# A graph attention kernel: score rows ordered by oct, attribute products as two 64-column tiles, weighted sums and transposes in one run each

## The chip, the cores and the metric

The kernel runs on one core of one Trainium2 chip. The metric is device time in microseconds. The kernel before takes 4986.42 us (median of 3 runs, 4981.60 to 4991.56). All numbers are fp32.

## The reference, cut to what matters

A graph of 6250 nodes and 206250 edges sorted by destination. One layer of attention over edges with 8 heads of 32 channels, then a feed-forward net, then a shared net and four gated experts.

```python
q, k, v = x @ Wq.T + bq, x @ Wk.T + bk, x @ Wv.T + bv       # per node, 8 heads x 32
e = edge_attr @ We.T                                        # per edge, from 64 attributes
alpha = sum(q[dst] * (k[src] + e), channels) / sqrt(32)     # 8 scores per edge
p = exp(alpha - segment_max(alpha, dst))
out = segment_sum((v[src] + e) * p, dst) / segment_sum(p, dst)
beta = sigmoid(concat(out, x_r, out - x_r) @ Wbeta.T)       # x_r: a skip projection
h = beta * x_r + (1 - beta) * out
x = layernorm(x + h); x = layernorm(x + gelu(x @ W1.T + b1) @ W2.T + b2)
y = x + shared_mlp(x) + gated top-2 of 4 experts
```

## The kernel before, in words

There are three stages. Stage 1 (to about 200 us) normalizes x, and makes for each node a row of keys and values in DRAM (`kv_rows`, 512 numbers) and columns of queries. Stage 2, the edge stage (about 200 to 3700 us), goes over 49 blocks of 128 nodes, and in each over GB = 8 steps of GN = 16 nodes. Stage 3 does everything behind the attention, row by row.

**One step of stage 2** has 16 nodes and their edges. The nodes are two octs of ON = 8; each oct (index `o`) has up to OW = 320 edges, so a step has 5 tiles of 128 edges. The edges' key and value rows are gathered by POOL, five indirect DMAs a step (L597), into one of four slots `F`; the edges' attributes and destination numbers come by SP's DMAs into `F3`.

TensorE does in a step:

- `scores` (L841, L844): for each half of the heads (index `c`) and each oct, 32 rows of scores (4 heads x 8 nodes) by 320 edges. Each is a product of queries with transposed keys `FT` and one of `G3` (queries times We) with the attributes `F3`, which also blanks edges of other nodes. The four row groups lie on four 32-wide column tiles of the array; in `pS` they stand at rows c*64 + o*32.
- `z_part` (L860), three times: for each of the four row groups the weights `PT` (32 columns) times 192 columns of `F`: 128 of values and the 64 attributes. To have these as one product for each half, the rows of `F` are laid out in blocks of 64: keys, a block of values, keys, values, values, values, attributes. It sums into `pZ`.
- `ft` (L828), three times: transposes of the keys of the step after the next, 4, 4 and 2, through the two buffers `ring`.
- `ea_rows` (L867): the next step's attributes with edges as rows. `pt` (L850): transposes of the weights `Pw`. `zt` (L873, L874): transposes of the sums `Zs` of the step, into `pZv` and `pZe`.

In step 1 of each block comes `project` (L881 to L887), in steps 2 and 5 `g3` (L818).

VectorE takes the maximum over `pS` (L656, L657), copies the transposed weights (L662), makes the blanking rows (L650), joins indices (L642), and twice a block takes `pZv` and `pZe` out (L678, L681). ScalarE copies `ring` to `FT` (L760), takes exp of the scores (L766), copies `pZ` to `Zs` (L807) and `pM` to `F` (L772). The order on each engine is written by hand, with semaphores between the engines: `ring_filled` and `ring_emptied` for ft, `s_done` for scores, `slot_free` for the last z of a step (POOL and SP start the loads of the next user of the slot on it), `z_out` for the copy of Z, `gathered` for a slot's rows.

## Time and profile before

| | |
|---|---|
| median of 3 runs | 4986.42 us (4981.60 to 4991.56) |
| profiled execution, whole time | 4956.95 us |
| its span | 4954.7 us |
| TensorE busy | 3986.7 us, 80% |
| VectorE, ScalarE, POOL busy | 1796.9, 1483.9, 1938.6 us |
| mean granted TensorE clock | 0.845 of full speed |
| gathers (L597) | 1970, 1894.3 us on POOL |

The profile is one execution of the program. A view in order of time gives start and length in us, the engine, the line of the kernel, the operation, the tiles written and read, shapes and the number of records put together; what stands in brackets is how long the engine had been idle and what released it. PE is TensorE, PEld its loads of weights, DVE VectorE, ACT ScalarE. A product in fp32 is two matmul records. The ends of TensorE's records are modelled.

### The profile page before, as it was taken

How to read it: one execution, taken by the hardware profiler on the slowest of the kernel's cores; microseconds unless marked ns; L12 is line 12 of the kernel's file. 1: busy time of each engine (PE TensorE's matmuls, PEld its weight loads, DVE VectorE, ACT ScalarE, POOL GpSimd, SP SyncE). 2: the span in 40 equal slices, each digit the busy share in tenths (PEclk: the TensorE clock that was granted, in tenths of full speed). 3: DMA queues.
4: the chain of work that ended last, by engine and by line, in shares of the span. 5: the costliest groups of instructions: out<-in, count | busy, mean ns of one | idle time of the engine just before them, and what ended most of it. 6: DMA issues, size and time to landing. Idle time of an engine off the chain costs nothing. (4 is left out here: it accounts for less than half of the span.)

```text
span 4954.7 us, 86461 instructions
## 1 busy us (share of the span) xinstructions
PE 3986.7 (80%) x28082; PEld 2157.7 (44%) x28082; DVE 1796.9 (36%) x4770; ACT 1483.9 (30%) x3644; POOL 1938.6 (39%) x2075
## 2 busy tenths in 40 slices
PE   6787888888888888888888888888867778778778
PEld 3344444444444444444444444444434445445445
DVE  5233333333333333333333333333335454544553
ACT  2133232222232233232332323223223323323322
POOL 2255555555555555555555555555530000000000
PEclk9788888888898888888889898888888778868877
DMA  5566666666666666666666666666660000000000
GB/s 191 161 180 179 172 172 172 175 170 169 181 179 172 168 176 170 173 174 173 173 171 182 178 183 179 172 171 177 170 165 18 15 15 15 15 15 15 15 15 7
DMA packets 638315, 665.65 MB, mean 134 GB/s; under 512 B 408275, under 2 KB 501908, under 8 KB 638244
## 3 DMA queue, kind: packets, MB, share of 16 engines
q0 software_dynamic: 159520, 523.41, 34.7%
q1 hardware_dynamic: 478740, 141.70, 13.9%
q14 instruction: 43, 0.35, 0.0%
q8 instruction: 12, 0.20, 0.0%
HBM read 632.59 MB, written 33.05 MB: 134 GB/s over the span
## 5 line engine op out<-in xcount | busy, mean ns | idle before, releaser
L597 POOL DMA_INDIRECT F<-kv_rows,srci x1970 | 1894.3, 962 | 1622.8 <-PE pZ L860 970.7
L760 ACT ACTIVATE FT<-ring 128x512 f32<-128x512 f32 (+1 forms) x1182 | 581.8, 526 | 1890.4 <-PE ring L828 1005.9
L828 PE MATMUL ring<-ident,F 128*128 128x128 f32 x3940 | 752.2, 309 | 407.8 <-ACT FT L760 392.5
L860 PE MATMUL pZ<-F,PT 128*32 128x192 f32 x9408 | 793.2, 362 | 117.6 <-issue 114.2
L828 PEld LDWEIGHTS ring<-ident,F 128*128 128x128 f32 x3940 | 447.1, 151 | 859.0 <-ACT FT L760 565.7
L656 DVE TENSOR_REDUCE nmx<-pS 128x1 f32<-128x384 f32 x393 | 219.3, 558 | 1263.3 <-remote 1098.9
L662 DVE COPY PT<-pPT 128x384 f32<-128x384 f32 x393 | 219.2, 558 | 956.6 <-issue 522.9
L860 PEld LDWEIGHTS pZ<-F,PT 128*32 128x32 f32 x9408 | 263.2, 116 | 483.0 <-issue 442.2
L1106 POOL DMA_DIRECT2D out_dram<-accb x6 | 5.8, 960 | 1077.8 <-DVEq L1271 1077.8
L841 PE MATMUL pS<-FT,qh 128*32 128x320 f32 x3144 | 382.6, 567 | 17.9 <-issue 14.2
L844 PE MATMUL pS<-F,G 80*32 80x320 f32 x3144 | 386.5, 571 | 0.0
L650 DVE TENSOR_SCALAR F<-F,nid 16x640 f32<-16x640 int32 x394 | 224.2, 569 | 41.5 <-issue 26.1
L850 PE MATMUL pPT<-ident,Pw 128*128 128x128 f32 x1179 | 236.0, 313 | 0.9 <-ACT Pw L766 0.9
L1382 PE MATMUL hid<-rT,W1T 128*128 128x512 f32 (+1 forms) x448 | 204.9, 617 | 35.6 <-ACT h L1314 27.9
L766 ACT ACTIVATE Pw<-pS,nMn 128x384 f32<-128x384 f32 x393 | 226.4, 576 | 7.6 <-DVE nMn L657 3.3
L778 ACT ACTIVATE G<-pM 64x512 f32<-64x512 f32 x99 | 58.6, 592 | 563.3 <-remote 380.6
L867 PE MATMUL pM<-ident,F 64*128 64x64 f32 x1965 | 213.5, 240 | 0.6
L844 PEld LDWEIGHTS pS<-F,G 80*32 80x32 f32 x3144 | 127.8, 140 | 171.9 <-issue 109.9
L1390 PE MATMUL nat<-W2T,h 128*128 128x256 f32 x784 | 176.3, 386 | 27.1 <-ACT h L1314 27.1
L867 PEld LDWEIGHTS pM<-ident,F 64*128 64x128 f32 x1965 | 158.2, 144 | 75.5 <-issue 75.5
L873 PE MATMUL pZv<-ident,Zs 128*128 128x128 f32 x392 | 137.8, 351 | 63.4 <-issue 55.0
L1287 ACT ACTIVATE rT<-tr 128x256 f32<-128x256 f32 x147 | 54.4, 384 | 436.8 <-PE tr L1373 434.9
(200 smaller groups left out, 4427.7 us busy)
## 6 DMA issues: line engine op xcount, KB each, us to landing
F<-in_edge_attrT SPq DMA_DIRECT2D x788, 80.0 KB
F<-kv_rows,srci POOLq DMA_INDIRECT x1970
F<-in_dst SPq DMA_DIRECT2D x788, 20.0 KB
srci<-src_front SPq DMA_DIRECT2D x796, 1.5 KB
kv_rows<-kvs SPq DMA_DIRECT2D x7, 1792.0 KB, 6.4
qb<-q_cols SPq DMA_DIRECT2D x100, 64.0 KB
U<-in_x SPq DMA_DIRECT2D x7, 896.0 KB, 10.9
xn_rows<-xs SPq DMA_DIRECT2D x7, 896.0 KB, 6.3
```

What stands on the lines that cost most here:

```text
L597: pool.indirect_dma_start(out=F[s][:, t, 0:KV], out_offset=None, in_=kv_d, in_offset=bass.IndirectOffsetOnAxis(ap=srci[j % GB][:, col:col ...
L650: dve.tensor_scalar(F3[j][DE:K3, :], F3[j][DE:K3, :].bitcast(I32), nid[DE:K3, c], None, ALU.not_equal).then_inc(neq_done, 1)
L656: ch.step(dve.tensor_reduce(nmx[:, j:j + 1], pS[:, 0:SW], AX.X, ALU.max, negate=True))
L662: dve.tensor_copy(PT[:, :, :], pPT[:, 0:SW].rearrange("p (t r) -> p t r", r=P)).then_inc(pt_emptied, 1)
L760: act.activation(FT[j % 2][:, :, t0 * P:t1 * P], ring[n % 2][:, 0:KD * w].rearrange("p (k e) -> p k e", e=w), ACT.Copy).then_inc(ring_empt ...
L766: act.activation(Pw[:, :], pS[:, 0:SW], ACT.Exp, bias=nMn[:, j:j + 1], accum_out=lsum[:, j:j + 1]).then_inc(p_done, 1)
L828: m = pe.transpose(ring[n % 2][:, k * w + (t - t0) * P:k * w + (t - t0 + 1) * P], F[j][:, t, k * 3 * BLK:k * 3 * BLK + P], ident[:, :])
L841: m = pe.matmul(pS[rows, cols], qh[half][:, c, g + o, :], FT[j % 2][:, c, o * OW:(o + 1) * OW], start=True, stop=False)
L844: m = pe.matmul(pS[rows, cols], G3[half][0:K3, c, g + o, :], F3[s][0:K3, o * OW:(o + 1) * OW], start=False, stop=True)
L850: m = pe.transpose(pPT[:, t * P:(t + 1) * P], Pw[:, t * P:(t + 1) * P], ident[:, :])
L860: m = pe.matmul(pZ[rows, 0:ZW].rearrange("p (x d) -> p x d", d=BLK), PT[:, t, rows], f, start=(t == 0), stop=(t == KB - 1))
L867: m = pe.transpose(pM[:, t * DE:(t + 1) * DE], F3[s][0:DE, t * P:(t + 1) * P], ident[0:DE, 0:DE])
```

## The change

Four things change together, and no arithmetic is left out.

- Row groups of scores, weights and sums stand at rows o*64 + c*32 in place of c*64 + o*32: first by oct, then by half of the heads. `seln`, `selh`, `G3`, the blanks and the reads of `pZv` and `pZe` follow.
- The two row groups of an oct are then neighbours and use the same attributes. The products with attributes, in `scores` and in `z_part`, are two on 64-wide column tiles in place of four on 32-wide ones. In `z_part` the values are four products of 128 columns, and the attributes two of 64 columns; before, both were in four of 192.
- The layout of a gathered row is keys (256), values (256), attributes (64), in place of blocks in turn, with fewer DMAs of weights and biases in stage 1.
- On TensorE all three `z_part` come first, then the three `ft`; the wait for gathered rows moves behind the sums. On ScalarE exp comes first, then the copy of `pZ`, then the three copies of `ring`.

```diff
--- before.py
+++ after.py
@@ -138,7 +137,7 @@
             nid = sbt(mid, "nid", [P, NG + 2])
-            G3 = [sbt(mid, f"G3{i}", [P, KD, HP // ON, C]) for i in range(2)]
+            G3 = [sbt(mid, f"G3{i}", [P, HP // ON, KD, C]) for i in range(2)]
             WeP = sbt(mid, "WeP", [P, HR, 2 * C])
@@ -205,16 +204,12 @@
                         wv = a["WvT"].rearrange("(k p) c -> p k c", p=P)
-                        for at, v0, v1 in ((2, 0, 1), (5, 1, 2), (6, 2, 4)):
-                            sp.dma_start(Wkv[:, :, at * BLK:(at + v1 - v0) * BLK], wv[:, :, v0 * BLK:v1 * BLK]).then_inc(wv_landed, 16)
-                            sp.dma_start(bkv[:, at * BLK:(at + v1 - v0) * BLK], a["bv"][v0 * BLK:v1 * BLK].partition_broadcast(P)
-                                         ).then_inc(bias_landed, 16)
+                        sp.dma_start(Wkv[:, :, D:KV], wv).then_inc(wv_landed, 16)
+                        sp.dma_start(bkv[:, D:KV], a["bv"].partition_broadcast(P)).then_inc(bias_landed, 16)
                         sp.dma_start(src_d[HP:], a["src"]).then_inc(src_stored, 16)
...
                         sp.wait_ge(bk_stored, 16)
-                        for o in range(KD):
-                            sp.dma_start(bkv[:, o * 3 * BLK:o * 3 * BLK + P], bk_d[o * P:(o + 1) * P].partition_broadcast(P)
-                                         ).then_inc(bias_landed, 16)
+                        sp.dma_start(bkv[:, 0:D], bk_d.partition_broadcast(P)).then_inc(bias_landed, 16)
                         sp.wait_ge(wep_cleared, 1)
@@ -279,7 +274,7 @@
                                         out=selh[:, c * HR:(c + 1) * HR], in_=selh[:, c * HR:(c + 1) * HR],
-                                        compare_op=ALU.not_equal, fill=1.0, base=-(c * HP + o * C + n),
+                                        compare_op=ALU.not_equal, fill=1.0, base=-(o * HP + c * C + n),
                                         pattern=[[-ON, HR]], channel_multiplier=1))
@@ -294,9 +289,11 @@
                                 for h in range(HR):
-                                    g3 = G3[i][:, :, :, :].rearrange("p c (g o) r -> p (c g) o r", o=2)[:, :, o, h * ON:(h + 1) * ON]
-                                    chp.step(pool.affine_select(out=g3, in_=g3, compare_op=ALU.not_equal, fill=-BIG, base=-(DE + o * ON),
-                                                                pattern=[[0, KD * HP // GN], [-1, ON]], channel_multiplier=1))
+                                    for c in range(KD):
+                                        g3 = G3[i][:, :, c, :].rearrange("p (g o) r -> p g o r", o=2)[:, :, o, h * ON:(h + 1) * ON]
+                                        chp.step(pool.affine_select(out=g3, in_=g3, compare_op=ALU.not_equal, fill=-BIG,
+                                                                    base=-(DE + o * ON), pattern=[[0, HP // GN], [-1, ON]],
+                                                                    channel_multiplier=1))
                         pool.sem_inc(sel_ready, 1)
@@ -621,9 +617,7 @@
                         for o in range(2):
-                            for c in range(KD):
-                                r = c * HP + o * C
-                                dve.memset(pS[r:r + C, (1 - o) * OW:(1 - o) * OW + HP], -BIG).then_inc(blank, 1)
+                            dve.memset(pS[o * HP:(o + 1) * HP, (1 - o) * OW:(1 - o) * OW + HP], -BIG).then_inc(blank, 1)
                         dve.memset(pZv[:, :], 0.0).then_inc(blank, 1)
@@ -676,10 +670,10 @@
                                 dve.tensor_copy(outT[rows, :, half, :].rearrange("p c (x n) -> p c x n", n=ON),
-                                                pZv[rows, :].rearrange("p (c x h n) -> p c x h n", c=KD, h=HR, n=ON)[:, :, :, h, :])
+                                                pZv[rows, :].rearrange("p (x c h n) -> p c x h n", c=KD, h=HR, n=ON)[:, :, :, h, :])
                             for c in range(KD):
                                 m = dve.tensor_copy(zeaT[c * DE:(c + 1) * DE, :, half, :].rearrange("p h (x n) -> p x h n", n=ON),
-                                                    pZe[0:DE, :].rearrange("p (c x h n) -> p c x h n", c=KD, h=HR, n=ON)[:, c, :, :, :])
+                                                    pZe[0:DE, :].rearrange("p (x c h n) -> p c x h n", c=KD, h=HR, n=ON)[:, c, :, :, :])
                             m.then_inc(copied, 1)
@@ -775,7 +769,8 @@
                             act.wait_ge(g3_filled, value)
-                            act.activation(G3[half][0:DE, :, :, :].rearrange("p c x r -> p (c x r)"), pM[0:DE, :], ACT.Copy
+                            act.activation(G3[half][0:DE, :, :, :].rearrange("p x c r -> p c x r"),
+                                           pM[0:DE, :].rearrange("p (c x r) -> p c x r", c=KD, r=C), ACT.Copy
                                            ).then_inc(g3_emptied, 1)
@@ -798,13 +793,12 @@
                                         g3_out(0, it * 2 + 3)
+                                    weights((j + 1) % GB, it * GB + (j + 2))
+                                    act.wait_ge(slot_free, it * GB + (SLOTS + j + 1))
+                                    act.activation(Zs[:, :], pZ[:, 0:ZW], ACT.Copy).then_inc(z_out, 1)
                                     for q in range(len(PAIRS)):
...
                                         ft_out(j, q, RING0 + m, rb + (m + 1))
-                                        if q == 0:
-                                            weights((j + 1) % GB, it * GB + (j + 2))
-                                    act.wait_ge(slot_free, it * GB + (SLOTS + j + 1))
-                                    act.activation(Zs[:, :], pZ[:, 0:ZW], ACT.Copy).then_inc(z_out, 1)
                                     ea_out((j + 1) % SLOTS, it * GB + (j + 2))
@@ -826,23 +820,21 @@
                                     m = pe.transpose(ring[n % 2][:, k * w + (t - t0) * P:k * w + (t - t0 + 1) * P],
-                                                     F[j][:, t, k * 3 * BLK:k * 3 * BLK + P], ident[:, :])
+                                                     F[j][:, t, k * P:(k + 1) * P], ident[:, :])
                             m.then_inc(ring_filled, 1)
...
                             half, g = j // HB, (j % HB) * 2
-                            for x in range(2):
-                                for c in range(KD):
-                                    for o in range(2):
-                                        r = c * HP + o * C
-                                        rows, cols = slice(r, r + C), slice(o * HP, o * HP + OW)
-                                        if x == 0:
-                                            m = pe.matmul(pS[rows, cols], qh[half][:, c, g + o, :],
-                                                          FT[j % 2][:, c, o * OW:(o + 1) * OW], start=True, stop=False)
-                                        else:
-                                            m = pe.matmul(pS[rows, cols], G3[half][0:K3, c, g + o, :],
-                                                          F3[s][0:K3, o * OW:(o + 1) * OW], start=False, stop=True)
+                            for c in range(KD):
+                                for o in range(2):
+                                    r = o * HP + c * C
+                                    pe.matmul(pS[r:r + C, o * HP:o * HP + OW], qh[half][:, c, g + o, :],
+                                              FT[j % 2][:, c, o * OW:(o + 1) * OW], start=True, stop=False)
+                            for o in range(2):
+                                m = pe.matmul(pS[o * HP:(o + 1) * HP, o * HP:o * HP + OW],
+                                              G3[half][0:K3, g + o, :, :].rearrange("p c r -> p (c r)"),
+                                              F3[s][0:K3, o * OW:(o + 1) * OW], start=False, stop=True)
                             m.then_inc(s_done, 1)
@@ -854,11 +846,12 @@
                                 for o in range(2):
-                                    rows = slice(c * HP + o * C, c * HP + (o + 1) * C)
-                                    blocks = F[s][:, o * TO + t, :].rearrange("p (x d) -> p x d", d=BLK)
-                                    f = blocks[:, 2:9:3, :] if c == 0 else blocks[:, 6:9, :]
-                                    m = pe.matmul(pZ[rows, 0:ZW].rearrange("p (x d) -> p x d", d=BLK), PT[:, t, rows], f,
-                                                  start=(t == 0), stop=(t == KB - 1))
+                                    rows = slice(o * HP + c * C, o * HP + (c + 1) * C)
+                                    pe.matmul(pZ[rows, 0:P], PT[:, t, rows], F[s][:, o * TO + t, D + c * P:D + (c + 1) * P],
+                                              start=(t == 0), stop=False)
+                            for o in range(2):
+                                rows = slice(o * HP, (o + 1) * HP)
+                                m = pe.matmul(pZ[rows, P:ZW], PT[:, t, rows], F[s][:, o * TO + t, KV:FP], start=False, stop=(t == KB - 1))
                             return m
@@ -869,9 +862,9 @@
 
-                            g = slice((j % HB) * HP, (j % HB + 1) * HP)
-                            pe.transpose(pZv[:, :].rearrange("p (c r) -> p c r", c=KD)[:, :, g], Zs[:, 0:P], ident[:, :])
-                            pe.transpose(pZe[0:DE, :].rearrange("p (c r) -> p c r", c=KD)[:, :, g], Zs[:, P:ZW], ident[:, :]).then_inc(zt_filled, 1)
+                            g = slice((j % HB) * P, (j % HB + 1) * P)
+                            pe.transpose(pZv[:, g], Zs[:, 0:P], ident[:, :])
+                            pe.transpose(pZe[0:DE, g], Zs[:, P:ZW], ident[:, :]).then_inc(zt_filled, 1)
 
@@ -941,12 +934,12 @@
                                         z = z_part(s, t)
-                                        if t == KB - 1:
-                                            z.then_inc(slot_free, 1)
-                                        if t == 0:
-                                            pe.wait_ge(gathered[s2], it * (16 * T * 2) + 16 * T * ((j + 2) // SLOTS + 1))
-                                        pe.wait_ge(ring_emptied, rb + (m + t - 1))
-                                        ft(s2, t, RING0 + m + t)
+                                    z.then_inc(slot_free, 1)
+
+                                    pe.wait_ge(gathered[s2], it * (16 * T * 2) + 16 * T * ((j + 2) // SLOTS + 1))
+                                    for q in range(len(PAIRS)):
+                                        pe.wait_ge(ring_emptied, rb + (m + q - 1))
+                                        ft(s2, q, RING0 + m + q)
                                     if j == 1:
```

TensorE's instructions for one step without extra work (step 3 of a block), before. `pS` are scores, `pZ` sums, `ring` the transposed keys, `pM` the attribute rows, `pPT` the transposed weights; 32x320 is a product's output.

```order
L841 MATMUL pS<-FT,qh 32x320 x4
L844 MATMUL pS<-F,G 32x320 x4
L860 MATMUL pZ<-F,PT 32x192 x4
...
L828 MATMUL ring<-ident,F 128x128 x4
L860 MATMUL pZ<-F,PT 32x192 x4
L828 MATMUL ring<-ident,F 128x128 x4
L860 MATMUL pZ<-F,PT 32x192 x4
...
L828 MATMUL ring<-ident,F 128x128 x2
L867 MATMUL pM<-ident,F 128x64 x5
L850 MATMUL pPT<-ident,Pw 128x128 x3
L873 MATMUL pZv<-ident,Zs 128x2x64
L874 MATMUL pZe<-ident,Zs 64x2x64
```

After:

```order
L832 MATMUL pS<-FT,qh 32x320 x4
L835 MATMUL pS<-F,G 64x320 x2
L850 MATMUL pZ<-F,PT 32x128 x4
L854 MATMUL pZ<-F,PT 64x64 x2
L850 MATMUL pZ<-F,PT 32x128 x4
L854 MATMUL pZ<-F,PT 64x64 x2
L850 MATMUL pZ<-F,PT 32x128 x4
L854 MATMUL pZ<-F,PT 64x64 x2
...
L822 MATMUL ring<-ident,F 128x128 x8
...
L822 MATMUL ring<-ident,F 128x128 x2
L860 MATMUL pM<-ident,F 128x64 x5
L842 MATMUL pPT<-ident,Pw 128x128 x3
L866 MATMUL pZv<-ident,Zs 128x128
L867 MATMUL pZe<-ident,Zs 64x128
```

Each z has its two attribute products behind the value products, the three z stand in one run, and eight of the ten transposes of keys follow in one run.

ScalarE's instructions of the same step, before:

```order
L760 ACTIVATE FT<-ring 128x2x256
L766 ACTIVATE Pw,lsum<-pS,nMn 128x384
...
L760 ACTIVATE FT<-ring 128x2x256
...
L760 ACTIVATE FT<-ring 128x2x128
...
L807 ACTIVATE Zs<-pZ 128x192
L772 ACTIVATE F<-pM 128x5x64
```

After:

```order
L760 ACTIVATE Pw,lsum<-pS,nMn 128x384
...
L798 ACTIVATE Zs<-pZ 128x192
...
L754 ACTIVATE FT<-ring 128x2x256
...
L754 ACTIVATE FT<-ring 128x2x256
...
L754 ACTIVATE FT<-ring 128x2x128
L766 ACTIVATE F<-pM 128x5x64
```

exp (`Pw`) and the copy of the sums (`Zs`) moved ahead of the copies of `ring` into `FT`.

## Rows read from the trace of the kernel before

**Rows 1.** The page's first line on busy time: engine, us, share of the span, instructions.

```profile
PE 3986.7 (80%) x28082; PEld 2157.7 (44%) x28082; DVE 1796.9 (36%) x4770; ACT 1483.9 (30%) x3644; POOL 1938.6 (39%) x2075
```

**Rows 2.** Busy time by stretch: the edge stage, and the step of rows 3 (clock granted).

```profile
800.00:3600.00 2800.00, 2325.42 (x20026) 1185.28 (x20019) 888.37 (x2495) 840.19 (x2338) 1526.16 (x1588) 0.87 0.64 174
...
2029.40:2043.00 13.60, 9.93 (x104) 5.26 (x104) 5.90 (x17) 4.94 (x14) 7.20 (x9) 1.00 0.65 179
```

**Rows 3.** TensorE in order of time, one step: start, length, line, operation, idle before.

```profile
2034.54 0.74 PE L841 MATMUL pS<-FT,qh 128*32 128x320 f32 x8
2035.10 0.72 PE L844 MATMUL pS<-F,G 80*32 80x320 f32 x8
2035.64 0.51 PE L860 MATMUL pZ<-F,PT 128*32 128x192 f32 x8
2036.08 0.66 PE L828 MATMUL ring<-ident,F 128*128 128x128 f32 x4
2036.66 0.53 PE L860 MATMUL pZ<-F,PT 128*32 128x192 f32 x8
...
2037.71 0.53 PE L860 MATMUL pZ<-F,PT 128*32 128x192 f32 x8
2040.87 0.44 PE L828 MATMUL ring<-ident,F 128*128 128x128 f32 x2 [2.62 <-ACT FT L760]
...
2041.69 0.55 PE L850 MATMUL pPT<-ident,Pw 128*128 128x128 f32 x3
2042.51 0.30 PE L873 MATMUL pZv<-ident,Zs 128*128 128x128 f32 x1 [0.27 <-issue]
...
2042.85 0.59 PE L841 MATMUL pS<-FT,qh 128*32 128x320 f32 x4
```

**Rows 4.** VectorE in order of time, the same step.

```profile
2037.32 0.56 DVE L656 TENSOR_REDUCE nmx<-pS 128x1 f32<-128x384 f32 x1 [2.09 <-PE pS L844]
2037.91 0.16 DVE L657 TENSOR_TENSOR nMn<-nmx,nMo 128x1 f32<-128x1 f32 x1
```

**Rows 5.** ScalarE in order of time, the same step.

```profile
2040.22 0.60 ACT L760 ACTIVATE FT<-ring 128x512 f32<-128x512 f32 x1 [5.78 <-remote]
2040.71 0.57 ACT L766 ACTIVATE Pw<-pS,nMn 128x384 f32<-128x384 f32 x1
2041.18 0.20 ACT L766 ACTIVATION_READ_ACCUMULATOR Pw<-pS,nMn 128x1 f32 x1
2041.27 0.87 ACT L760 ACTIVATE FT<-ring 128x512 f32<-128x512 f32 x2
2042.01 0.35 ACT L807 ACTIVATE Zs<-pZ 128x192 f32<-128x192 f32 x1
```

**Rows 6.** POOL in order of time, the first gather after the same step's sums.

```profile
2041.29 0.94 POOL L597 DMA_INDIRECT F<-kv_rows,srci  x1 [2.24 <-remote]
```

**Rows 7.** The page's costliest groups: the maximum, one for each step.

```profile
L656 DVE TENSOR_REDUCE nmx<-pS 128x1 f32<-128x384 f32 x393 | 219.3, 558 | 1263.3 <-remote 1098.9
```

**Rows 8.** Groups by line and shape, 800 to 3600 us: busy, mean ns, idle before.

```profile
L656 DVE TENSOR_REDUCE nmx<-pS 128x1 f32<-128x384 f32 x317 | 176.9, 558 | 1022.7 <-remote 908.1 <-PE pS L844 78.3 <-issue 36.3
...
L884 PE MATMUL pM<-WeP,zeaT 128*128 128x64 f32 x320 | 56.3, 339 | 0.0
...
L874 PEld LDWEIGHTS pZe<-ident,Zs 128*64 128x64 f32 x317 | 40.2, 127 | 0.0
```

**Rows 9.** All engines in order of time, a step whose scores are delivered late.

```profile
1349.76 0.75 PE L841 MATMUL pS<-FT,qh 128*32 128x320 f32 x8
...
1355.45 0.56 DVE L656 TENSOR_REDUCE nmx<-pS 128x1 f32<-128x384 f32 x1 [3.85 <-remote]
1355.57 0.60 ACT L760 ACTIVATE FT<-ring 128x512 f32<-128x512 f32 x1 [5.90 <-PE ring L828]
...
1358.74 0.76 PE L841 MATMUL pS<-FT,qh 128*32 128x320 f32 x4
```

**Rows 10.** POOL in order of time, its first long wait at the start.

```profile
90.49 1.64 POOL L305 MEMSET U<- 128x1848 f32 x1 [10.69 <-DVE xs L344]
```

14 lines of the change are left out of this document (6 added, 8 removed).

## The prediction

> **What bounds the kernel now.** I read the page's shares first: TensorE is busy for 80% of the span, every other engine under 40% [rows 1]. The stretch 800 to 3600 us is all edge stage; DMA engines are busy 64% there, POOL 55% [rows 2]. So neither moves all the time, and the question is what TensorE's stretch of one step consists of. The edge stage is 392 steps of 16 nodes (393 maxima with the one ahead of the loop [rows 3]); 317 of them lie in 2800 us, 8.83 us each on average [rows 2, 4], so it is seven tenths of the time.
>
> Next I read one step in order of time without extra work, at the full clock [rows 2, 5]. Scores start at 2034.54 and the next scores at 2042.85: 8.31 us. TensorE's records of scores and the three weighted sums (z) with two runs of row transposes between them (ft) end by 2038.24, 3.7 us after the start. Then it stands still for 2.62 us and goes on with the third ft, edge rows, transposes of the weights (pt) and of the sums (zt), and the next scores. What it waits for is ScalarE's copy of the first ft, which starts at 2040.22 [rows 6]. So ScalarE's first copy is in the chain. It wasn't late because of other work on ScalarE: ScalarE had been idle for 5.78 us.
>
> The third reading is how late the other engines see what TensorE's records call finished. The score records end at 2035.82, and DVE's maximum, which waits for nothing else, starts at 2037.32 [rows 7]: 1.5 us later. The first ft's records end at 2036.74, and the copy starts 3.5 us later. POOL, which waits for the last z (records end 2038.24), goes on at 2041.29 [rows 8]. After transposes alone there is no such gap: pt ends at 2042.24 and its copy on DVE follows at once. So the column-tiled products deliver late, and results come together: the copy of ft at 2040.22 and POOL's restart are a microsecond apart though a z, an ft and another z lie between. I call the stretch from the start of scores to 2040.22 the head (5.68 us) and the rest the tail (2.63 us).
>
> By the Trainium skill (Perfetto Trace Analysis, Tensor Engine Instruction), TensorE's end in a profile is estimated from the instruction's size, not observed. The trace agrees: after tiled products, waiting engines start 1.5 to 3.5 us behind that end. So I size the head by when others start, not by TensorE's busy time.
>
> The tail: the ft copy (0.60) lets the third ft start at 2040.87; then edge rows; pt 2041.69; zt at 2042.51, held 0.27 us for the copy of Z, which starts at 2042.01 because exp and the three ft copies are ahead of it [rows 5, 6].
>
> **The change part by part**, per step.
>
> Term 1, z products. Before, each of three z is four products of 192 columns on 32-wide tiles, each run as two matmuls (eight records). After, it is four of 128 columns and two of 64 columns on 64-wide tiles: twelve records. Four records of 320 columns side by side take a quarter of 2034.54 to 2035.64, 0.275 us [rows 5], 0.86 ns a column. Sixty-four fewer columns in two rounds save 0.11 us per z, 0.33 in all. The added products: at least the same columns on two tiles, 0.11 per z, net 0. At most each of four stands alone for 0.18 us, what a 64-column matmul with full-width weights takes (56.3 us by 320 [rows 4]): 0.70 per z, net +1.8. The nearest row for the weights is the 64-wide load, 0.127 us [rows 4]; two rounds of that, pairs side by side, are 0.26 per z: net +0.45. I take this. The score products against the attributes go from four to two on 64-wide tiles with the same 320 columns, so two rounds stay two rounds: nothing.
>
> Term 2, changes between tile shapes. z to ft start to start takes 0.44 us for 192 columns in two rounds, 0.33 by the above; ft to the next z 0.58 for four transposes of 0.11 (four last 0.66, three of pt 0.55): 0.11 to 0.15 us lost at each change, 0.13 on average. Between scores and third ft there are five changes. After: if 32-wide to 64-wide counts as a change, there are eight (two around the attribute scores, five within z, one to ft): +3, +0.39. If it doesn't, only one is left: -4, -0.5. No row shows 32 against 64. I take +0.39, since the weights of the one shape occupy the array that the other needs.
>
> The Trainium skill (TensorEngine Tiling (Array Packing), Key Properties) says that a change of the tiling mode, not just of the tile, drains TensorE. The trace agrees for 32 to 128 wide, 0.13 us each; by the rule 32 to 64 would cost likewise, which is the upper of the two counts and speaks against this change.
>
> Term 3, order in the head. Before, the ft copy comes as late as the whole run z, ft, z, ft, z. After, it needs three z and one ft; the second ft runs beside ScalarE's copies of Z (0.35) and of the first ft (0.60). One ft of 0.58 us leaves the head: -0.58 at best. At worst nothing, if the late delivery sets the head. I take -0.58.
>
> Term 4, tail. ScalarE now does exp, Z copy, three ft copies. The Z copy waits for the last z and runs beside the first ft. zt no longer waits: -0.27. pt doesn't wait either, exp being long done. In the tail edge rows and pt stay in the chain.
>
> Term 5, late scores. exp (ready 0.75 after the maximum starts, then 0.67 with its read) now stands ahead of every ft copy. In the step shown the maximum starts at 2037.32 and exp would be over at 2038.8, before the last z is delivered: free. But there are steps where scores are delivered with everything else [rows 9]: scores from 1349.76, maximum at 1355.45, ft copy at 1355.57, next scores 1358.74. There exp runs behind the first copy today. After, the minimum is ready at 1356.20, exp with its read at about 1356.9, Z copy 1357.24, ft copy 1357.84 instead of 1356.17: +1.67, and from there 1.75 instead of 2.57: net +0.85. DVE's mean wait ahead of the maximum is 3.23 us over 317 steps (1022.7 us), between the 2.09 of the first step and 3.85 of the late one [rows 4, 7, 9]. After, 36 tiled matmul records follow the scores with nothing between; before, transposes came after eight. I see no reason why scores be delivered earlier, some why later, and count half of the steps: +0.45. Ends 0 and +0.85.
>
> The rest: POOL's 16 added selects at the start run ahead of a wait of 10.69 us for x rows [rows 10], which would have to grow past that to show; covered. Eight DMAs of weights and biases become three; the matmuls of that stage wait for the rows of x longer. The gathers wait for the last z and are needed two steps on: 6.3 us of issue in 8.3 leave room, and TensorE asks for them later than before. Strided reads on DVE and ScalarE keep their sizes. Stage 3 is the same code.
>
> Sum: +0.45 +0.39 -0.58 -0.27 +0.45 = +0.44 us a step, by 392 steps +172 us. The profiled execution is 4956.95 us (span 4954.7), 29 below the median 4986.42 of the runs: 5129 against the profile, 5158 against the runs. I say 5150.
>
> **The rivals.**
> - Faster, order alone counts: 32 against 64 is no change of mode and the added products hide at their columns: 0 -0.5 -0.58 -0.27, with late steps at +0.45: -0.9 us a step, at most -350 us; if delivery, not issue, sets the head, half of it, about 4800. For it: TensorE stands 2.62 us in wait of a copy. Against: that copy isn't late through order, but through delivery. It decides from the point at which the six z and attribute groups cost under 0.15 us a step more than today.
> - Slower by the count of tiled products: the head is the same in slow and fast steps where records are 3.7 us long, as if each tiled matmul had a price in delivery. There are 40 in the 5.68 us, 0.14 each; after, 48: +1.1 us a step, +445, about 5420. For it: results come late only behind tiled products. Against: maybe width counts, and the 64-wide ones are fewer bytes.
> - No change: the head is set by something outside (gathers' traffic beside it) and what the tail wins the late steps lose: 4986.
>
> **How the numbers follow.** My forecast, slower by one to six per cent: 0.5. Count of tiled products: 0.17. Faster: 0.25. No change: 0.08. What a measurement can tell from no change is 0.2%, 10 us. So faster 0.25, same 0.07, slower 0.68. The likeliest case's own range is 5030 to 5300. The range that holds 8 in 10 goes from 4840 (leaving out the best of the faster case) to 5400.
>
> **What would show it.** In the profile after: the step without extras at 8.7 to 8.8 us, from 8.3; the first attribute product of z 0.13 us or more behind the records' columns (term 2); twelve records per z in about 0.75 us (terms 1 and 2); ScalarE in the order exp, Z, ft; zt right behind pt (term 4); steps in which Z's copy begins right behind exp (term 5). I am wrong if z with its attribute products takes no longer than today, or if ScalarE's first ft copy begins earlier than 5.5 us after the scores.

## The result and the profile after

The changed kernel takes 5033.26 us (median of 4 runs, 5024.53 to 5035.17) against 4984.01 us of before on the same chip (4959.93 to 4991.56): ratio 1.0104, 95% interval 1.0067 to 1.0140. It is slower, as forecast, but by 49 us where I had forecast 166. Measured again on another chip (e9 below), both kernels were equal (1.0010, 0.9993 to 1.0027).

Groups of rows are named here by the numbers under which they stand above. (The prediction numbers six of them otherwise: its 3 is Rows 7, its 4 is Rows 8, its 5 is Rows 3, its 6 is Rows 5, its 7 is Rows 4, its 8 is Rows 6.)

The page's first line, after; [rows 1] of before. The span is 5022.5 us, 67.8 longer.

```profile
PE 4135.4 (82%) x31214; PEld 2452.8 (49%) x31214; DVE 1795.1 (36%) x4768; ACT 1597.7 (32%) x3644; POOL 1945.9 (39%) x2091
```

Busy time by stretch, after: the edge stage, then two steps that follow each other. Columns as in [rows 2]: stretch and length; TensorE, its loads, VectorE, ScalarE, POOL; clock, DMA share, GB/s.

```profile
800.00:3600.00 2800.00, 2390.27 (x22120) 1396.85 (x22123) 871.80 (x2451) 918.46 (x2301) 1500.90 (x1558) 0.88 0.63 171
...
2014.10:2023.00 8.90, 7.35 (x80) 3.92 (x80) 4.29 (x14) 2.78 (x8) 4.90 (x6) 1.00 0.63 173
2023.00:2032.00 9.00, 7.54 (x64) 4.50 (x66) 3.79 (x11) 2.83 (x7) 4.64 (x6) 0.81 0.62 167
```

TensorE is busy 65 us longer in the 2800 us, with fewer steps done; the clock and the traffic stayed. TensorE in order of time, after, a step without extra work at the full clock; it answers to [rows 3].

```profile
2014.14 0.75 PE L832 MATMUL pS<-FT,qh 128*32 128x320 f32 x8
2014.82 0.76 PE L835 MATMUL pS<-F,G 80*64 80x320 f32 x4
2015.51 0.43 PE L850 MATMUL pZ<-F,PT 128*32 128x128 f32 x8
2015.86 0.34 PE L854 MATMUL pZ<-F,PT 128*64 128x64 f32 x4
2016.13 0.42 PE L850 MATMUL pZ<-F,PT 128*32 128x128 f32 x8
2016.48 0.34 PE L854 MATMUL pZ<-F,PT 128*64 128x64 f32 x4
2016.90 0.27 PE L850 MATMUL pZ<-F,PT 128*32 128x128 f32 x1
2017.65 0.27 PE L850 MATMUL pZ<-F,PT 128*32 128x128 f32 x1 [0.48 <-issue]
2018.36 0.45 PE L850 MATMUL pZ<-F,PT 128*32 128x128 f32 x6 [0.44 <-issue]
2018.74 0.34 PE L854 MATMUL pZ<-F,PT 128*64 128x64 f32 x4
2019.01 1.09 PE L822 MATMUL ring<-ident,F 128*128 128x128 f32 x8
2020.64 0.44 PE L822 MATMUL ring<-ident,F 128*128 128x128 f32 x2 [0.55 <-ACT FT L754]
2021.01 0.52 PE L860 MATMUL pM<-ident,F 64*128 64x64 f32 x5
2021.46 0.55 PE L842 MATMUL pPT<-ident,Pw 128*128 128x128 f32 x3
2021.85 0.27 PE L866 MATMUL pZv<-ident,Zs 128*128 128x128 f32 x1
...
2022.16 0.75 PE L832 MATMUL pS<-FT,qh 128*32 128x320 f32 x8
```

This step takes 8.02 us, less than the 8.31 of [rows 3]; the next one, at a mean clock of 0.81 of full speed (partly at 1.2 GHz), 9.58. One step is no mean, which matters below. The first two sums start 0.62 us apart (2015.51, 2016.13), where z to ft took 0.44. The scores take 1.37 us to the first sum, 1.10 before. Then TensorE issues single records some 0.7 us apart, until 2018.36: the stop that stood behind the third z is now within it.

VectorE, ScalarE and POOL in order of time, the same step; [rows 4 to 6].

```profile
2018.42 0.56 DVE L650 TENSOR_REDUCE nmx<-pS 128x1 f32<-128x384 f32 x1 [1.88 <-remote]
```

```profile
2019.21 0.58 ACT L760 ACTIVATE Pw<-pS,nMn 128x384 f32<-128x384 f32 x1 [5.39 <-DVE nMn L651]
2019.69 0.19 ACT L760 ACTIVATION_READ_ACCUMULATOR Pw<-pS,nMn 128x1 f32 x1
2019.78 0.32 ACT L798 ACTIVATE Zs<-pZ 128x192 f32<-128x192 f32 x1
2019.99 1.51 ACT L754 ACTIVATE FT<-ring 128x512 f32<-128x512 f32 x3
```

```profile
2016.29 0.95 POOL L593 DMA_INDIRECT F<-kv_rows,srci  x1 [0.30 <-issue]
2019.97 0.94 POOL L593 DMA_INDIRECT F<-kv_rows,srci  x1 [2.73 <-PE pZ L854]
```

The first of the two is the last of the five gathers that POOL had begun behind the step before. The same one of the kernel before, in the step of [rows 3]:

```profile
2038.10 0.94 POOL L597 DMA_INDIRECT F<-kv_rows,srci  x1 [0.30 <-issue]
```

The score records end at 2015.58 and the maximum starts 2.84 us later. ScalarE now waits for it; the copy of Z begins right behind exp, and the first ft copy after that, 5.85 us behind the start of the scores (5.68 before).

Groups by line, after, 800 to 3600 us: the maximum ([rows 8]), exp and the copy of Z.

```profile
L650 DVE TENSOR_REDUCE nmx<-pS 128x1 f32<-128x384 f32 x312 | 174.0, 558 | 956.6 <-remote 840.9 <-PE pS L835 110.1 <-issue 5.6
...
L760 ACT ACTIVATE Pw<-pS,nMn 128x384 f32<-128x384 f32 x312 | 180.7, 579 | 1269.6 <-DVE nMn L651 1083.9 <-issue 178.8
...
L798 ACT ACTIVATE Zs<-pZ 128x192 f32<-128x192 f32 x312 | 100.9, 323 | 73.2 <-PE pZ L854 72.2
```

VectorE's wait ahead of the maximum is 3.07 us a step (3.23 before). The copy of Z waits only 0.23 us a step; in 224 of the 312 steps it begins right behind exp, where I had counted such a delay in half of the steps.

### The profile page after: what moved, and what is told of

The parts are those of the page before. It is cut to its first block and busy times, and to the rows that moved or that the text cites. A ratio compares the mean times of both kernels' runs of the same rounds, so it can differ in the third digit from the quotient of the medians.

```text
span 5022.5 us, 92750 instructions
## 1 busy us (share of the span) xinstructions
PE 4135.4 (82%) x31214; PEld 2452.8 (49%) x31214; DVE 1795.1 (36%) x4768; ACT 1597.7 (32%) x3644; POOL 1945.9 (39%) x2091
## 5 line engine op out<-in xcount | busy, mean ns | idle before, releaser
L850 PE MATMUL pZ<-F,PT 128*32 128x128 f32 x9408 | 668.3, 296 | 251.4 <-issue 245.8
L822 PEld LDWEIGHTS ring<-ident,F 128*128 128x128 f32 x3940 | 526.0, 168 | 245.4 <-ACT FT L754 185.6
L854 PE MATMUL pZ<-F,PT 128*64 128x64 f32 x4704 | 476.0, 257 | 160.5 <-issue 157.9
L850 PEld LDWEIGHTS pZ<-F,PT 128*32 128x32 f32 x9408 | 247.2, 110 | 581.2 <-issue 529.2
L854 PEld LDWEIGHTS pZ<-F,PT 128*64 128x64 f32 x4704 | 276.7, 143 | 436.9 <-issue 431.9
L832 PE MATMUL pS<-FT,qh 128*32 128x320 f32 x3144 | 327.8, 493 | 1.2 <-issue 0.7
L835 PE MATMUL pS<-F,G 80*64 80x320 f32 x1572 | 321.3, 489 | 0.0
L860 PE MATMUL pM<-ident,F 64*128 64x64 f32 x1965 | 236.5, 259 | 0.0
L860 PEld LDWEIGHTS pM<-ident,F 64*128 64x128 f32 x1965 | 177.4, 161 | 89.8 <-issue 89.8
L835 PEld LDWEIGHTS pS<-F,G 80*64 80x64 f32 x1572 | 82.0, 142 | 235.6 <-issue 235.6
```

What stands on the lines that cost most here:

```text
L822: m = pe.transpose(ring[n % 2][:, k * w + (t - t0) * P:k * w + (t - t0 + 1) * P], F[j][:, t, k * P:(k + 1) * P], ident[:, :])
L832: pe.matmul(pS[r:r + C, o * HP:o * HP + OW], qh[half][:, c, g + o, :], FT[j % 2][:, c, o * OW:(o + 1) * OW], start=True, stop=False)
L835: m = pe.matmul(pS[o * HP:(o + 1) * HP, o * HP:o * HP + OW], G3[half][0:K3, g + o, :, :].rearrange("p c r -> p (c r)"), F3[s][0:K3, o * OW ...
L850: pe.matmul(pZ[rows, 0:P], PT[:, t, rows], F[s][:, o * TO + t, D + c * P:D + (c + 1) * P], start=(t == 0), stop=False)
L854: m = pe.matmul(pZ[rows, P:ZW], PT[:, t, rows], F[s][:, o * TO + t, KV:FP], start=False, stop=(t == KB - 1))
L860: m = pe.transpose(pM[:, t * DE:(t + 1) * DE], F3[s][0:DE, t * P:(t + 1) * P], ident[0:DE, 0:DE])
```

## The experiments

Eighteen runs in five groups, each group on one chip beside the kernel before. "Mean step" is the time from one step's scores to the next in the trace (360 to 383 steps, 300 to 3650 us): of all, of the five of a block without extra work, of the three with `project` or `g3`. The first line is the result itself.

| kernel | median us | ratio to before (95%) | mean step: all / without / with extra |
|---|---|---|---|
| before | 4984.01 | 1 | 8.81 / 8.46 / 9.38 |
| changed | 5033.26 | 1.0104 (1.0067–1.0140) | 8.97 / 9.04 / 8.87 |
| e1 old tiles, both new orders | 4845.04 | 0.9783 (0.9756–0.9810) | 8.52 / 8.44 / 8.64 |
| e2 new tiles, both old orders | 5110.54 | 1.0310 (1.0272–1.0348) | 9.26 / 9.16 / 9.41 |
| e3 ScalarE's new order alone | 5030.87 | 1.0169 (1.0138–1.0200) | 8.97 / 8.72 / 9.40 |
| e4 TensorE's new order alone | 4796.87 | 0.9707 (0.9672–0.9743) | 8.39 / 8.26 / 8.60 |
| e9 changed again | 4945.91 | 1.0010 (0.9993–1.0027) | 8.77 / 8.87 / 8.59 |
| e10 = e4 again | 4800.06 | 0.9705 (0.9690–0.9721) | 8.37 / 8.25 / 8.57 |
| e11 attribute sums together | 4894.70 | 0.9893 (0.9871–0.9915) | 8.64 / 8.65 / 8.63 |
| e12 two ft ahead of the sums | 4871.53 | 0.9845 (0.9831–0.9860) | 8.60 / 8.35 / 9.02 |
| e13 changed, ScalarE's old order | 4871.26 | 0.9845 (0.9832–0.9859) | 8.58 / 8.48 / 8.74 |
| e14 changed, scores 32-wide | 5000.25 | 1.0100 (1.0083–1.0116) | 8.93 / 9.01 / 8.80 |
| e15 changed, sums 32-wide | 4962.81 | 1.0025 (1.0001–1.0049) | 8.80 / 8.91 / 8.62 |
| e16 before, one gather a step | 3768.94 | 0.7616 (0.7604–0.7628) | 5.76 / 5.26 / 6.59 |
| e17 sums of 192 columns, ScalarE's old order | 4816.54 | 0.9665 (0.9636–0.9694) | 8.48 / 8.26 / 8.84 |
| e18 sums of 192 columns | 4947.76 | 0.9939 (0.9916–0.9962) | 8.74 / 8.44 / 9.24 |

e5 to e8 ran on a chip on which the kernel before takes 4081.66 us; they stand apart below. e1 to e4 shared a chip (before 4953.85), e9 to e12 another (4947.48), e13 to e16 a third (4948.54); e17 and e18 ran later on that one (4977.84). Ratios of different groups are compared below; where two such ratios differ by less than about 1%, I don't read the difference, since e9 and the first line are the same kernel and differ by 0.9%.

**Orders against tiles.** e1 takes both of these parts from the change, e4 TensorE's alone, e3 ScalarE's alone; e2 is the changed kernel with both undone.

```diff
 TensorE:
-for t in range(KB): z_part(s, t); (t == 0: wait gathered); ft(s2, t)
+for t in range(KB): z_part(s, t)
+wait gathered
+for q in range(3): ft(s2, q)
 ScalarE:
-ft copy 0, exp, ft copy 1, ft copy 2, wait slot_free, Zs<-pZ
+exp, wait slot_free, Zs<-pZ, ft copies 0, 1, 2
```

Expected of e1: 

> The kernel before with the two orders of the change (TensorE: three z, then three ft; ScalarE: exp, copy of Z, ft copies), tiles and layout as before. Theory A, the order is what costs: exp stands ahead of the ft copies in steps whose scores are delivered late, 0.85 us in some of them, so this kernel is slower than before by all of the change's 49 us or more, 5030 to 5080. Rival B, the tiles cost (64-wide products in between 32-wide ones) and the order gains, since one ft leaves the chain and zt waits no more: faster than before, 4880 to 4970.

Of e2: 

> The changed kernel with both orders put back (z and ft in turn; first ft copy, exp, the other ft copies, copy of Z); row order, layout and the 64-wide attribute products stay. Theory A (order costs): about as before, 4960 to 5000. Rival B (tiles cost): slower than the changed kernel, 5050 to 5150, because between every two ft there are two more changes of tile shape.

Of e3: 

> The kernel before with ScalarE's order alone changed (exp, copy of Z, then the ft copies). TensorE's order is as before, so the first ft copy additionally waits for the last z, exp and the copy of Z. Theory A: this alone is the loss, 5050 to 5200, as ft copies are 0.35 us later in each step and 1.7 us in late ones. Rival B: as ft and z are delivered together anyway, 0 to +30 us.

Of e4: 

> The kernel before with TensorE's order alone changed (z, z, z, then ft, ft, ft); ScalarE as before (first ft copy, exp, two ft copies, copy of Z). If three z in one run lengthen nothing, the first ft copy comes as late as now and time is unchanged within 20 us (both theories allow it); if delivery of scores is held by a run of tiled products without transposes between, the steps get longer, +50 us or more; if changes between tile shapes cost 0.13 us each, four fewer give -200 us.

TensorE's order gains 2.9%, ScalarE's loses 1.7% alone and 0.8% behind TensorE's (e1 against e4), the tiles lose 3.1%. So the change joins a gain with two losses. Of the expectations only one held: e2 lies where rival B had it. e1 is faster than both of its ranges, e3 with +77 us lies between its two, and e4's -157 us is nearest to the price for changes of tile shape, which later runs don't bear out.

**The same on a quick chip.** e5, e6 and e7 are the changed kernel with one edit:

```diff
 e5, scores:
-for o: pe.matmul(pS[o*HP:(o+1)*HP, ...], G3[..., g+o] as 64 columns, F3)
+for c: for o: pe.matmul(pS[r:r+C, ...], G3[..., g+o, c, :], F3)
 e6, z_part:
-for o: pe.matmul(pZ[o*HP:(o+1)*HP, P:ZW], ...)
+for c: for o: pe.matmul(pZ[o*HP+c*C:o*HP+(c+1)*C, P:ZW], ...)
 e7: the 12 value products of a step, then the 6 attribute products
 e8 (before): POOL gathers one tile of five in the loop
```

In e8 four slots are filled whole ahead of the loop, and most edges then use rows of earlier steps: it leaves out four fifths of the gathers.

Expected of e5: 

> The changed kernel with the attribute scores on four 32-wide tiles again (the attribute products of z stay two on 64-wide tiles). Two of eight changes of tile shape a step go. Theory S, a change of shape between 32 and 64 wide costs about 0.13 us: 2 by 0.13 by 392 = 100 us faster than the changed kernel, 4900 to 4930. Rival N, the number of tiled products counts (48 records a step become 52): 20 to 80 us slower than it, 5020 to 5090.

Of e6: 

> The changed kernel with the attribute products of z on four 32-wide tiles of 64 columns (eight records in place of four for each z), scores as changed. Six changes of shape a step go to one, 12 more records come. Theory S: at least 5 by 0.13 by 392 = 250 us faster than the changed kernel, about 4750, if the records themselves are free. Rival N (records count, 0.14 us each by the prediction's sum): 12 more, +600 us, 5600; a result near the changed kernel's would say that both weigh alike.

Of e7: 

> The changed kernel with the 12 value products of a step's z first and then the six 64-wide attribute products, same records, in place of value and attribute products in turn. Changes of shape within z go from six to two. Theory S: 4 by 0.13 by 392 = 200 us faster than the changed kernel, 4790 to 4840. Rival N: unchanged, within 15 us of it, since the number of records is the same.

Of e8: 

> The kernel before with one of the five gathers of a step in the loop (four slots are filled whole ahead of it); so most edges use the rows of earlier steps, and the gathered traffic and POOL's work fall to a fifth. It asks what delays the delivery of tiled products. Theory D, the gathers' traffic does: VectorE's wait ahead of the maximum falls from 3.2 us a step to under 1.5, and the kernel takes 4000 to 4500 us. Rival E, it lies in the tiled products themselves at the full clock: the wait stays at 3 us and the time within 2% of before.

Medians 4008.84, 3971.53, 3971.30 and 3763.94 us; ratios 0.9826 (0.9786–0.9865), 0.9740 (0.9701–0.9780), 0.9738 (0.9699–0.9777) and 0.9228 (0.9180–0.9276). The mean step of e7 is 6.32 us. Its window of the edge stage, the maximum there, and TensorE in one step:

```profile
800.00:2600.00 1800.00, 1642.69 (x20277) 1052.56 (x20279) 801.18 (x2255) 847.87 (x2105) 1364.63 (x1428) 1.00 0.86 244
```

```profile
L650 DVE TENSOR_REDUCE nmx<-pS 128x1 f32<-128x384 f32 x286 | 159.5, 558 | 83.1 <-PE pS L835 79.5
```

```profile
2006.87 0.86 PE L853 MATMUL pZ<-F,PT 128*32 128x128 f32 x24
2007.66 0.57 PE L858 MATMUL pZ<-F,PT 128*64 128x64 f32 x12
2008.16 1.09 PE L822 MATMUL ring<-ident,F 128*128 128x128 f32 x8
```

VectorE waits 0.29 us a step ahead of the maximum here, not 3: the scores aren't delivered late. POOL starts its 1428 gathers 1.26 us apart with pauses of 0.30 us, so five take 6.30 us, and they bound the step. So this chip couldn't tell the terms apart in time, and e8 couldn't test what makes delivery late. It does show one price of issue: the three z of e7 take 1.29 us to the first ft, and three of 0.62 us would take 1.86, so four changes of tile width fewer save 0.57 us, 0.14 each. The kernel before wasn't profiled on this chip.

**Again where delivery is late.** e9 is the changed kernel, e10 is e4, e11 is e7. e12 is before with this order on TensorE (ScalarE: ft, ft, exp, ft, Z):

```diff
-z_part 0, ft 0, z_part 1, ft 1, z_part 2, ft 2
+ft 0, ft 1, z_part 0, z_part 1, z_part 2, ft 2
```

Expected of e9: 

> The changed kernel itself, once more. The same kernel before took 4954 us on one chip and 4082 us on another, where VectorE waits 0.2 us ahead of the maximum in place of 3.2. Where results of tiled products are delivered late, the ratio to before should be 1.010 again. Where they aren't, theory S (changes of shape cost what the records show) and the order's gain leave it below before: e5 and e6, which differ from it by two and five changes of shape, were at 0.983 and 0.974, so 0.98 to 1.00.

Of e10: 

> The kernel before with TensorE's order alone changed, which was at 0.971 of before on a chip with late delivery. On such a chip again 0.971. On one without, POOL's five gathers (6.27 us a step) bound the step, and it comes to 0.97 too, like e7 (3971 us), by another cause; theory S says not above 0.98 on either.

Of e11: 

> The changed kernel with the values of all three z first and then their attribute products (e7), for the other kind of chip. With late delivery theory S says 200 us faster than the changed kernel (four changes of shape a step), a ratio to before of 0.96 to 0.975; theory N (the number of tiled records counts there) says the same as the changed kernel, 1.00 to 1.015.

Of e12: 

> The tiles of before, with the first two runs of transposes ahead of the three z and the third behind them; ScalarE copies the first two, then does exp, the third copy and the copy of Z. The third ft then waits for no copy and the first copy starts about 2 us earlier. Where the first ft copy is in the chain (late delivery) faster than e10: 0.94 to 0.97. If the delivery of everything behind the scores is held until the window of tiled products has drained, it is the same as e10, 0.97. Where gathers bound, the same as e10 within 0.5%.

e10 repeats e4 to 0.0002. e11, with four changes of tile shape fewer, is 51 us faster than the changed kernel, 0.03 us a change; that lies between its two theories. The changed kernel was expected at 1.010 again and came at 1.001. In e12, ft ahead of the sums is worse than behind them (0.9845 against 0.9705), outside all that I had expected of it, and the runs don't say why.

**Which tile edit, and ScalarE's order with new tiles.** e13 is the changed kernel with ScalarE's old order, e14 is e5, e15 is e6, e16 is e8.

Expected of e13: 

> New tiles, TensorE's new order, ScalarE's old order. If the two parts add (order of TensorE alone 0.971 of before, new tiles alone +3.1%): about 1.00. If ScalarE's new order costs what it cost with the old tiles (+1 to +1.7%), this is 0.985 to 0.99 of before where the changed kernel is 1.00 to 1.01. If the tiles' cost lies where the old order changes shape twelve times and not in the z run, it is 0.975 or less.

Of e14: 

> The changed kernel with its attribute scores on four 32-wide tiles again: two changes of shape fewer a step. My term: -0.26 us a step, 100 us, 0.98 of the changed kernel. By the grouping run (four changes fewer, -51 us): -25 us, 0.995. Rival, price by matmuls: two matmuls more, +50 us.

Of e15: 

> The changed kernel with its attribute sums on four 32-wide tiles of 64 columns: six changes fewer a step, six matmuls more. By my terms -0.78 us a step, at most -300 us. By the grouping run -75 us. Rival, price by matmuls: at least +150 us.

Of e16: 

> The kernel before with one of five gathers a step in the loop; most edges then use rows of earlier steps. If the gathers' traffic is what makes scores arrive late, VectorE's mean wait ahead of the maximum falls from 3.2 us to under 1 and the time to 0.85 or less. If it is not, the wait stays above 2.5 us and the time at 0.97 or more.

e13 beats the changed kernel by 1.65% (0.9845 against e9's 1.0010) and loses 1.4% to e10. In this order of taking parts ScalarE's order is the larger loss; by e1 and e4 it was 0.8%, and the tiles then 2.3 to 3.3% (e9 and the first line against e1). Which of the two is larger depends on what else is in place. TensorE in order of time in e14:

```profile
2002.67 0.75 PE L832 MATMUL pS<-FT,qh 128*32 128x320 f32 x8
2003.23 0.72 PE L837 MATMUL pS<-F,G 80*32 80x320 f32 x8
2003.77 0.40 PE L851 MATMUL pZ<-F,PT 128*32 128x128 f32 x8
```

and in e15:

```profile
2000.24 0.45 PE L850 MATMUL pZ<-F,PT 128*32 128x128 f32 x8
2000.48 0.33 PE L855 MATMUL pZ<-F,PT 128*32 128x64 f32 x8
2000.59 0.43 PE L850 MATMUL pZ<-F,PT 128*32 128x128 f32 x8
2000.81 0.33 PE L855 MATMUL pZ<-F,PT 128*32 128x64 f32 x8
2001.07 1.09 PE L822 MATMUL ring<-ident,F 128*128 128x128 f32 x8
```

In e14 the scores take 1.10 us again, 0.27 less than with two 64-wide products: 0.13 us for each of two changes of tile width. In e15 a z takes 0.35 us, and 0.48 with the change to ft behind it, not 0.62. Neither shortened the kernel: 1.0100 and 1.0025, where the changed one has 1.0010 to 1.0104. So the time doesn't pay for TensorE's issue in the head one for one. Both forecasts for e14 and both for e15 missed. e14 is 54 us slower than e9, close to the 50 of the price by matmuls, but on another chip; e15, of which that price asked at least 150, is 17 us slower.

e16, the kernel before with a fifth of the gathers, in the same views: window, the maximum's group, TensorE, VectorE, ScalarE. Its edge stage ends at 2486 us, so the window is shorter.

```profile
800.00:2400.00 1600.00, 1587.96 (x17512) 893.37 (x17508) 768.93 (x2188) 763.12 (x2051) 263.42 (x278) 1.00 0.39 85
```

```profile
L658 DVE TENSOR_REDUCE nmx<-pS 128x1 f32<-128x384 f32 x278 | 155.0, 558 | 71.1 <-PE pS L846 70.0
```

```profile
2003.34 0.75 PE L843 MATMUL pS<-FT,qh 128*32 128x320 f32 x8
2003.91 0.72 PE L846 MATMUL pS<-F,G 80*32 80x320 f32 x8
...
2008.50 0.48 PE L843 MATMUL pS<-FT,qh 128*32 128x320 f32 x4
```

```profile
2004.70 0.56 DVE L658 TENSOR_REDUCE nmx<-pS 128x1 f32<-128x384 f32 x1 [0.27 <-PE pS L846]
```

```profile
2005.58 0.60 ACT L762 ACTIVATE FT<-ring 128x512 f32<-128x512 f32 x1 [2.34 <-PE ring L830]
```

The wait ahead of the maximum is 0.26 us (3.23 with all gathers), the first ft copy comes 2.24 us behind the start of the scores (5.68), and the step takes 5.16 us (8.31) with the same products in the same order. TensorE is busy for 99% of the window. Without most of the gathers this chip and the quick one are alike: 3768.94 and 3763.94 us. So the gathers make delivery late. e16 takes away their transfers and POOL's work of issuing them together, so it doesn't say which of the two.

**The split of the sums.** e18 is the changed kernel with rows laid out in blocks and a z of four products of 192 columns, as before; e17 has ScalarE's old order as well.

```diff
-values: 4 x 128 columns (32-wide), attributes: 2 x 64 columns (64-wide)
+4 x 192 columns (32-wide), F in blocks of 64 as before
```

TensorE in e17, the three sums in one run and the first ft behind them:

```profile
2000.46 1.18 PE L859 MATMUL pZ<-F,PT 128*32 128x192 f32 x24
2001.58 0.66 PE L829 MATMUL ring<-ident,F 128*128 128x128 f32 x4
```

Expected of e17: 

> The sums with their attributes in one product of 192 columns as before (rows laid out as before); attribute scores on two 64-wide tiles, rows by oct, TensorE's new order, ScalarE's old order. With new sums this was 0.9845 of before, with old tiles throughout 0.9705. If the sums' split costs the 70 us between them: 0.970 here. If the attribute scores do: 0.984. Per my term 1 the sums' split costs +0.45 us a step, and this would be 0.95 of before.

Of e18: 

> The same with ScalarE's new order, so the changed kernel but for the split of the sums. The changed kernel was 1.001 to 1.010 of before, the new orders with old tiles 0.978. If the split makes the difference: 0.978 to 0.99. If it is the attribute scores: 1.00.

The split costs 1.8% with ScalarE's old order (e13 against e17), by the ratios some 89 us or 0.23 us a step; the two medians, from different groups on one chip, are 55 us apart. Without it, e17 is at e10's level (0.9665 and 0.9705, in different groups), near the 0.970 that was expected if the split costs; there the 64-wide scores cost nothing that I can show. With ScalarE's new order they do: e18 is 1.6% above e1 (0.9939 and 0.9783, on different chips), and outside both ranges expected of it. e18 against e17 gives ScalarE's order 131 us. e17 and e4/e10 beat both kernels; which of the two is better stays open.

## Why the forecast had the sign and not the size

The parts don't add up in one way. Three walks through the mean steps lead from before (8.81) to the changed kernel (8.97, or 8.77 in the second trace, whose differences stand in brackets).

| part, us a step | through e4, e13 | through e4, e1 | through e2, e13 | forecast |
|---|---|---|---|---|
| tiles | +0.19 | +0.45 (+0.25) | +0.45 | +0.84 |
| TensorE's order | -0.42 | -0.42 | -0.68 | -0.58 |
| ScalarE's order | +0.39 (+0.19) | +0.13 | +0.39 (+0.19) | +0.18 |

Each sums to +0.16 or -0.04, by 392 steps +63 or -16 us. On every walk the tiles are what was sized most wrongly.

- **Terms 1 and 2 (tiles), +0.84: the step that failed.** It failed in two places.
  - As issue of TensorE, term 2 was right: about 0.13 us for each change, eight for five, +0.39. Term 1 was not. In e17 three z of 192 columns in a run take 1.12 us to the first ft, one change among it, so 0.33 each; the 0.62 of the changed z has two changes in it and leaves 0.36. The added products cost 0.03 us a z, 0.1 a step, and not the +0.45 that I took from a row on loads of weights. "Twelve records per z in about 0.75 us" came as 0.62.
  - Of this issue the time pays a part. From e4 to e13 the tiles add seven changes and the 0.1, some 1.0 us of issue, and the mean step grows by 0.19; from before to e2 they add 0.78 (0.27 in the scores, 0.17 in each z), and it grows by 0.45. e14 and e15 show it from the other side: 0.27 and some 0.7 us a step of issue taken out, nothing gained. I had put the whole of it on the path, though my own reading was that the head is set by late delivery and must be sized by when others start. By the Trainium skill (TensorEngine Tiling (Array Packing), Key Properties) a change of mode drains TensorE; the trace agrees that 32 to 64 wide loses time as 32 to 128 does, 0.13 us each, but the kernel's time shows 0.03 us of it in e11.
- **The path, which I had wrong too.** Of the gathers I wrote that 6.3 us of issue in 8.3 leave room. In the traces they don't. In all 340 steps of before between 400 and 3400 us POOL issues its five gathers in one run of 6.0 us, then stands until the last z is delivered, 2.78 us on average; 6.0 and 2.8 are the mean step. In 271 steps of before ScalarE had waited over 1 us for its first ft copy, and in none of them did the copy start while such a run went on; the median start is 1.23 us behind the run's end (1.03 to 1.40 in eight of ten). In the step of [rows 3] the fifth gather ends at 2039.04 and the copy starts at 2040.22, and in the changed kernel the fifth ends at 2017.24 and the maximum starts at 2018.42: 1.18 us both times. So most results look held until the gathers are out, and what lengthens the step is what is still missing of z at that time. POOL's mean stand is 2.32 us in e4, 2.42 in e17, 2.41 in e13, 2.53 in e1, 2.93 in the changed kernel and 3.21 in e2, nearly in step with the mean steps. In the step shown only two of the third z's twelve records are out before 2018.36, and POOL stands 2.73 us; in the step of before all three z were out by 2038.24, and it stood 2.25. That this is how the tiles cost their part is my reading of one step each, and that the gathers hold the results is argued from these times and from e16; no run moved or stretched the gathers alone. Some results do get through during the run: 247 of the 340 maxima of before start within it.
- **Term 3 (order on TensorE), -0.58:** right in kind, -0.42 to -0.68. Its 0.58 for one ft contains a change of tile shape (0.44 without), which term 2 had already taken out, so my sum counted that 0.14 twice. The gain isn't even over the steps: -0.20 without extra work, -0.78 with `project` or `g3` (e4).
- **Terms 4 and 5 (ScalarE), -0.27 and +0.45, net +0.18:** right in sign; measured +0.13 with the old tiles (e4 to e1), +0.19 and +0.39 with the new ones. I had counted half of the steps, and exp delays the copy of Z in 224 of 312. zt does stand right behind pt (2021.46, 2021.85), as term 4 said.
- **By 392 steps.** I worked out one step without extra work. For those the measured difference is +0.58 (8.46 to 9.04; +0.41 in the second trace), with +0.44 forecast; the three others of a block gain 0.51 (9.38 to 8.87), and I hadn't looked at one. Five by 0.58 less three by 0.51, over eight, is +0.17. The tiles cost +0.22 to +0.70 in steps without extra work, and -0.05 to +0.23 in those with. Even where the +0.44 fits, it does so by luck: a tile term too large beside an order term of -0.58 that gives -0.20 there.
- **The rivals.** "Order alone counts" named about 4800 us; that is what TensorE's order gives alone (4796.87, 4800.06), with tiles and ScalarE's order left out. "A price for each tiled product" falls: e15 runs six products a step more than the changed kernel in nearly the same time. "No change" had eight in a hundred and came true on one chip. The first half of its reason, a head set by the gathers, is what e16 and the runs of gathers bear out; the second, that the tail wins what the late steps lose, isn't: a gain from TensorE's order cancels two losses. My two conditions for being wrong held off: z is longer, the first ft copy isn't earlier than 5.5 us. They tested issue and one step, and couldn't catch this miss.

Open: the split of the sums costs 89 us with ScalarE's old order and, by e18 (0.9939) against the changed kernel (1.0010 to 1.0104), 0.7 to 1.6% with the new one. Why e14 and e15 gain nothing, though e18 does, I can't say. The granted clock moves too, and not with the time: from 800 to 3400 us it is 0.87 before, 0.90 in e4, 0.97 in e13, 0.87 in e17, which is the fastest. I didn't run a kernel with all parts at one clock.

## What to carry to other kernels

Where others see an engine's results microseconds after its records end, added work on that engine is worth only what it moves of those results: size it by when the waiting engines start, in all terms. Look also at what an engine that seems to have room is doing at the moment when results come: here POOL, idle a third of each step, closed the loop. Work out the steps with extra work too, and look there first when a mean disagrees with the step that was read. Test the parts of a bundled change one at a time: here one of three (TensorE's order, 0.9705) held all the gain. Test them in more than one order, since the price of a part hung on the others.

## What the runs showed of the hardware

- The gathers make TensorE's column-tiled products deliver late, on some chips: with a fifth of them the maximum's wait falls from 3.23 to 0.26 us and the kernel to 0.76. Whether it is their traffic or POOL's issuing isn't shown. It isn't the rate of either by itself: on the quick chip e7 moves 244 GB/s, against 174 [rows 2], with POOL issuing a gather each 1.26 us, and the maximum waits 0.29 us. By the Trainium skill (SBUF — State Buffer, SBUF: two separate sides) a compute operation and a DMA cannot slow each other in SBUF; the runs don't show through which resource they meet here, so they neither bear this out nor refute it.
- Where delivery is late, ScalarE's first copy of ft starts 1.23 us (median of 271 steps, before) behind the end of POOL's five gathers, and never during them; the maximum of the changed kernel 1.25 us behind (253 of 334 steps).
- The kernel before takes 4081.66 us on one chip and 4947 to 4984 on others; with a fifth of the gathers 3763.94 and 3768.94.
- A change between 32-wide and 64-wide column tiles costs 0.13 to 0.14 us of TensorE's issue (e14 and e7 against the changed kernel), about the same as between 32 and 128.
- While results are late, TensorE doesn't stop at once: in the step shown it issues 37 records from the start of the scores on, and then single ones some 0.7 us apart (2016.90, 2017.65, 2018.36).
